# Moving the gate logits, the normalised rows and their stores from a stage of their own into the attention units

## What is computed

```python
x = x + _L1_xattn_ref(_layernorm(x), ctx_1024, ctx_1024, W_Query, W_Key, W_Value, W_Output, ...)
xf = _layernorm(x).reshape(N, D)               # N = 4096 tokens, D = 256
probs = softmax(xf @ gate_w.T)                 # 8 gate logits per token
scores_sel = _xmoe_route(probs)                # needs the probabilities of all tokens
y_e = gelu(xf @ w1[e].T) @ w2[e].T             # for each expert, capacity 512 tokens
x = x + sum over e of scores_sel[:, e] * y_e
```

## Time and profile before

| what | us |
|---|---|
| median of 3 runs (1861.0 to 1865.55) | 1862.72 |
| the profiled execution | 1861.19 |
| its span | 1859.5 |
| TensorE busy (91% of the span) | 1683.3 |
| VectorE busy (64%) | 1192.0 |
| ScalarE busy (45%) | 842.8 |
| GpSimd busy (33%) | 619.9 |

### The profile page before, as it was taken

One profiled execution on the slowest core, in us unless ns is written; L12 is line 12 of the kernel. 1 busy time (PEld: TensorE's weight loads), 2 busy tenths in 40 slices (PEclk: granted clock), 3 DMA queues, 4 the chain that ended last, 5 costly groups with the idle time before them and its releaser, 6 DMA issues. The chain is left out here.

```text
span 1859.5 us, 26060 instructions
## 1 busy us (share of the span) xinstructions
PE 1683.3 (91%) x8890; PEld 1152.6 (62%) x8890; DVE 1192.0 (64%) x2642; ACT 842.8 (45%) x1870; POOL 619.9 (33%) x746
## 2 busy tenths in 40 slices
PE   6469999996999999999999999999999999873584
PEld 4357777764666666666666666666666666572352
DVE  6444454432777777777777777777777777667761
ACT  3324443431555555555555555555555555421110
POOL 2154444430333232333333233232323232210375
PEclk9669999997999999999999999999999999955797
DMA  7100000003323222232323223232322223144144
GB/s 258 21 22 13 12 12 1 1 0 105 69 46 69 53 61 64 51 69 46 69 48 67 56 58 68 46 69 46 68 51 64 58 57 69 23 146 132 44 85 57
DMA packets 66657, 109.46 MB, mean 59 GB/s; under 512 B 16088, under 2 KB 48096, under 8 KB 66528
## 3 DMA queue, kind: packets, MB, share of 16 engines
q1 hardware_dynamic: 60384, 99.29, 21.8%
q0 software_dynamic: 6144, 8.52, 2.8%
HBM read 27.84 MB, written 12.85 MB: 22 GB/s over the span
## 5 line engine op out<-in xcount | busy, mean ns | idle before, releaser
L1030 POOL TENSOR_SCALAR at_Pr<-at_Pr,at_rinv 128x512 f32<-128x512 f32 x512 | 354.1, 692 | 826.7 <-DVE at_rinv L1057 826.7
L1009 ACT ACTIVATE at_Pr<-at_ps,at_nmax 128x512 f32<-128x512 f32 x512 | 352.0, 687 | 522.7 <-DVE at_nmax L1052 521.1
L1052 DVE TENSOR_REDUCE at_nmax<-at_ps 128x1 f32<-128x512 f32 x512 | 350.9, 685 | 139.0 <-PE at_ps L917 128.0
L917 PE MATMUL at_ps<-at_k,at_q 128*128 128x512 f32 x1024 | 420.8, 492 | 9.7 <-DMA at_k<-at_k_own 8.0
L928 PE MATMUL at_ps<-k_ident,at_Pr 128*128 128x128 f32 x2048 | 310.5, 274 | 4.0 <-POOL at_Pr L1030 4.0
L928 PEld LDWEIGHTS at_ps<-k_ident,at_Pr 128*128 128x128 f32 x2048 | 249.5, 140 | 93.2 <-POOL at_Pr L1030 32.8
L1064 DVE COPY at_PT<-at_ps 128x512 f32<-128x512 f32 x384 | 261.3, 681 | 0.0
L917 PEld LDWEIGHTS at_ps<-at_k,at_q 128*128 128x128 f32 x1024 | 174.6, 191 | 129.6 <-issue 120.1
L938 PE MATMUL at_ps<-at_PT,at_V 128*64 128x512 f32 x1024 | 233.8, 598 | 0.9 <-DVE at_PT L1064 0.9
L1057 DVE RECIPROCAL at_rinv<-at_rsum 128x1 f32<-128x1 f32 x512 | 83.3, 163 | 174.5 <-ACT at_Pr L1009 172.5
L938 PEld LDWEIGHTS at_ps<-at_PT,at_V 128*64 128x64 f32 x1024 | 67.7, 136 | 121.5 <-issue 120.3
(11 more groups left out here) (237 smaller groups left out, 2030.5 us busy)
## 6 DMA issues: line engine op xcount, KB each, us to landing
at_k<-at_k_own SPq DMA_DIRECT2D x256, 256.0 KB, 4.1
k_x<-in_x SPq DMA_DIRECT2D x8, 512.0 KB, 7.8
mg_ctx<-in_ctx SPq DMA_DIRECT2D x8, 512.0 KB, 8.0
mx_ctxn<-in_ctx SPq DMA_DIRECT2D x8, 512.0 KB, 3.9
rows<-lo_xn SPq DMA_DIRECT2D x8, 512.0 KB, 3.0
out<-k_x SPq DMA_DIRECT2D x1, 4096.0 KB, 14.6
r_w<-in_L_ffn_w SPq DMA_DIRECT2D x16, 256.0 KB, 5.6
mx_w<-in_L_ffn_w SPq DMA_DIRECT2D x2, 1024.0 KB, 9.8
```

The source lines that it names most:

```text
L917: ins = pe.matmul(ps[:, S_BANK + j % 2, :], q2[:, u % 2, h, q:q + P], k2[:, u % 2, h, part, :], start=part == 0, stop=part == 1)
L1009: act.activation(Pr[:, j % 4, :], ps[:, S_BANK + j % 2, :], ACT.Exp, bias=nmax[:, j % 4:j % 4 + 1], accum_out=rsum[:, j % 4:j % 4 + 1]).th ...
L1030: pool.tensor_scalar(Pr[:, n % 4, :], Pr[:, n % 4, :], rinv[:, n % 4:n % 4 + 1], 1.0, ALU.mult, ALU.mult).then_inc(s["pn"], 1)
L1052: dve.tensor_reduce(nmax[:, j % 4:j % 4 + 1], ps[:, S_BANK + j % 2, :], AX.X, ALU.max, negate=True).then_inc(s["nmax"], 1)
```

## The change

The block logits is gone. Its work for batch b is done in the units of batch b+1: routed(u, r) gives the batch whose step belongs to unit u, which is b = u // 8 - 1 if u % 8 == r. In unit 8b+9 (NORM) VectorE takes the statistics in slots 2 to 5 and finishes them in slot 6, and GpSimd the power after its last tile. In unit 8b+10 (APPLY) VectorE normalises in slots 2 to 5, into the part of ctxT_all that batch b no longer needs (semaphore xn). In unit 8b+11 (TURN) TensorE turns the rows in slots 3 and 7, into A_BANK + 1. ScalarE copies them in slot 4 and in slot 0 of the next unit. In unit 8b+12 (GATE) TensorE makes the gate matmuls in slots 3 and 7, and ScalarE copies the logits in slot 0 of the unit after. The key projection of two units gets a wait for these copies.

The SP queue stores the normalised rows of a batch and its part of out (two DMAs of 256 KB and one of 512 KB, waiting for xn) in its loop, at unit 8b+11. The gate weights are loaded already transposed, by two DMAs with one piece of 4 bytes per weight, where they were loaded by rows and turned by TensorE. The last batch has no units behind it, and its steps follow the loop. The zeros of the spare rows are made and stored in router, and experts waits for the semaphores of all stores (rows_in, landed).

```diff
-def attention(nc, c, x_all, xnT_all, ctxT_all, first, Wq, Wk, Wv, Wo):
+def attention(nc, c, x_all, xnT_all, ctxT_all, first, Wq, Wk, Wv, Wo, gate_w, lg, rows, rows_in, out, landed):
...
         rinv = sb("rinv", [P, 4], F32)
+        gT = sb("gT", [P, DC, E], F32)
+        stats = sb("stats", [P, TPB, 6], F32)
+        mv = sb("mv", [P, TPB, 2], F32)
+        ve = sb("ve", [P, TPB], F32)
+        rstd = sb("rstd", [P, TPB], F32)
-                 "pt_v pt_a pv oT y_ps x")
+                 "pt_v pt_a pv oT y_ps x gT stats mv ve rstd xn tx_ps xT l_ps lg")
...
             return 0 <= u < U
+        def routed(u, r):
+            return u // HP - 1 if u >= HP and u % HP == r else None
+        NORM, APPLY, TURN, GATE, LAST = 1, 2, 3, 4, B - 1
+        def x_tile(b, t):
+            return x_all[:, b * TPB + t:b * TPB + t + 1, :].rearrange("p a d -> p (a d)")
+        def xn_tile(b, t):
+            at = b * S + D * (t % 2)
+            return ctxT_all[:, t // 2, at:at + D]
...
                 sp.dma_start(wo_s[:, :, :], wo_dram).then_inc(first["loaded"], 16)
+                with nc.allow_non_contiguous_dma("8 gate weights per row"):
+                    for k in range(DC):
+                        sp.dma_start(gT[:, k, :], gate_w.rearrange("e (k p) -> p k e", p=P)[:, k, :]
+                                     ).then_inc(s["gT"], 16)
+                def store_rows(b):
+                    sp.wait_ge(s["xn"], b + 1)
+                    rv = rows.rearrange("(b k h p) d -> b p k h d", k=2, h=2, p=P)
+                    for k in range(2):
+                        sp.dma_start(rv[b, :, k, :, 0:D], ctxT_all[:, k, b * S:b * S + S].rearrange(
+                            "p (h d) -> p h d", d=D)).then_inc(rows_in, 16)
+                    sp.dma_start(out[0:N, :].rearrange("(b t p) d -> b p t d", p=P, t=TPB)[b],
+                                 x_all[:, b * TPB:(b + 1) * TPB, :]).then_inc(landed, 16)
                 for u in range(U):
+                    if routed(u, TURN) is not None:
+                        store_rows(routed(u, TURN))
...
                                          k_own[AD * h:AD * h + AD, :, :].bitcast(F32)).then_inc(s["k2"], 16)
+                store_rows(LAST)
...
                         wait_count(pe, s["kl"], u)
+                        if routed(u - 1, GATE) is not None:
+                            pe.wait_ge(s["xT"], DC * routed(u - 1, GATE) + DC)
+                        if routed(u - 1, GATE + 1) is not None:
+                            pe.wait_ge(s["lg"], routed(u - 1, GATE + 1) + 1)
...
                     ins.then_inc(s["y_ps"], 1)
+                def turn_rows(b, k):
+                    if k == 0:
+                        pe.wait_ge(s["xn"], b + 1)
+                    else:
+                        pe.wait_ge(s["xT"], DC * b + 1)
+                    for t in range(TPB):
+                        ins = pe.transpose(ps[:, A_BANK + 1, P * t:P * t + P], xn_tile(b, t)[:, P * k:P * k + P],
+                                           c["ident"][:, :])
+                    ins.then_inc(s["tx_ps"], 1)
+                def map_gates(b, half):
+                    if half == 0:
+                        pe.wait_ge(s["xT"], DC * b + DC)
+                    for t in (2 * half, 2 * half + 1):
+                        for k in range(DC):
+                            ins = pe.matmul(ps[:, A_BANK + 1, E * t:E * t + E],
+                                            xnT_all[:, k, b * S + P * t:b * S + P * t + P], gT[:, k, :],
+                                            start=k == 0, stop=k == DC - 1)
+                    if half:
+                        ins.then_inc(s["l_ps"], 1)
...
                             output(u - 1, j - 5)
+                        if j in (3, 7) and there(u):
+                            if j == 3 and there(u + 1) and u % HP in (TURN, GATE):
+                                pe.wait_ge(s["kl"], u + 2)
+                            if routed(u, TURN) is not None:
+                                turn_rows(routed(u, TURN), j // 4)
+                            if routed(u, GATE) is not None:
+                                if routed(u, GATE) == 0 and j == 3:
+                                    pe.wait_ge(s["gT"], 16 * DC)
+                                map_gates(routed(u, GATE), j // 4)
+                for k in range(DC):
+                    turn_rows(LAST, k)
+                for half in range(2):
+                    map_gates(LAST, half)
...
                                    ).then_inc(s["oT"], 1)
+                def keep_rows(b, k):
+                    act.wait_ge(s["tx_ps"], DC * b + k + 1)
+                    act.copy(xnT_all[:, k, b * S:b * S + S], ps[:, A_BANK + 1, :]).then_inc(s["xT"], 1)
+                def keep_logits(b):
+                    act.wait_ge(s["l_ps"], b + 1)
+                    act.copy(lg[:, b * TPB:(b + 1) * TPB, :],
+                             ps[:, A_BANK + 1, 0:TPB * E].rearrange("p (t e) -> p t e", e=E)).then_inc(s["lg"], 1)
...
                                            ).then_inc(s["exp"], 1)
+                        if j == 4 and routed(u, TURN) is not None:
+                            keep_rows(routed(u, TURN), 0)
+                        if j == 0 and routed(u, TURN + 1) is not None:
+                            keep_rows(routed(u, TURN + 1), 1)
+                        if j == 0 and routed(u, GATE + 1) is not None:
+                            keep_logits(routed(u, GATE + 1))
...
                                      ).then_inc(s["pt_a"], 1)
+                for k in range(DC):
+                    keep_rows(LAST, k)
+                keep_logits(LAST)
...
             def _(pool):
+                def spread(b):
+                    wait_apart(pool, s["ve"], b + 1)
+                    pool.tensor_tensor(rstd[:, :], ve[:, :], c["minus_half"][:, 0:TPB], ALU.pow
+                                       ).then_inc(s["rstd"], 1)
...
                                        ALU.mult, ALU.mult).then_inc(s["pn"], 1)
+                    if n % NBL == NBL - 1 and routed(n // NBL, NORM) is not None:
+                        spread(routed(n // NBL, NORM))
+                spread(LAST)
...
                     dve.tensor_tensor(xv, ps[:, Y_BANK - half, :], xv, ALU.add).then_inc(s["x"], 1)
+                def take_stats(b, t):
+                    if t == 0:
+                        dve.wait_ge(s["x"], 2 * HP * (b + 1))
+                    ins = dve.bn_stats(stats[:, t, :], x_tile(b, t))
+                    if t == TPB - 1:
+                        ins.then_inc(s["stats"], 1)
+                def finish_stats(b):
+                    wait_apart(dve, s["stats"], b + 1)
+                    for t in range(TPB):
+                        ins = dve.bn_aggr(mv[:, t, :], stats[:, t, :])
+                    ins.then_inc(s["mv"], 1)
+                    dve.wait_ge(s["mv"], b + 1)
+                    wait_count(dve, s["rstd"], b)
+                    dve.tensor_scalar(ve[:, :], mv[:, :, 1], LN_EPS, None, ALU.add).then_inc(s["ve"], 1)
+                def apply(b, t):
+                    if t == 0:
+                        dve.wait_ge(s["rstd"], b + 1)
+                    ins = dve.tensor_scalar(xn_tile(b, t), x_tile(b, t), mv[:, t, 0:1], rstd[:, t:t + 1],
+                                            ALU.subtract, ALU.mult)
+                    if t == TPB - 1:
+                        ins.then_inc(s["xn"], 1)
...
                                 keys(u + 1)
+                        if 2 <= j < 2 + TPB and routed(u, NORM) is not None:
+                            take_stats(routed(u, NORM), j - 2)
+                        if j == 2 + TPB and routed(u, NORM) is not None:
+                            finish_stats(routed(u, NORM))
+                        if 2 <= j < 2 + TPB and routed(u, APPLY) is not None:
+                            apply(routed(u, APPLY), j - 2)
...
                                 add_out(u - 1, 1)
+                for t in range(TPB):
+                    take_stats(LAST, t)
+                finish_stats(LAST)
+                for t in range(TPB):
+                    apply(LAST, t)
...
...
-def logits(nc, c, landed, x_all, gate_w, rows, lg, out, zeros):
...
-def router(nc, c, lg, rows, prob, chunk, slot_b, ew, w1T, w2T, prefetch):
+def router(nc, c, landed, out, zeros, lg, rows, prob, chunk, slot_b, ew, w1T, w2T, prefetch):
...
                 prefetch(sp)
+                sp.wait_ge(s["zero"], 1)
+                sp.dma_start(out[N:N + SPARE, :], zeros[:, :]).then_inc(landed, 16)
...
+                dve.memset(zeros[:, :], 0.0).then_inc(s["zero"], 1)
...
+                pool.wait_ge(rows_in, 16 * 2 * B)
...
-                pool.wait_ge(landed, 32)
+                pool.wait_ge(landed, 16 * (B + 1))
...
-            logits(nc, c, landed, x_all, a["L1_ffn_gate_w"], rows, lg, out, zeros)
```

(15 more changed lines are left out.)

115 lines of the change are left out of this document (removed).

## The result

The changed kernel takes 1911.25 us (median of 4, 1907.8 to 1912.07), the kernel before, run beside it on the same chip, 1861.86 us (median of 4, 1860.43 to 1865.55). The ratio is 1.0259, with a 95% interval of 1.0239 to 1.0279: the change makes the kernel 2.6% slower. The profiled execution took 1911.29 (span 1909.6) against 1861.19 (span 1859.5), so 50.1 us of span have to be found.

The account below looks back on a forecast made before the run. TensorE's pace was taken to bound the 64 attention units. From 1861.2 us, -37.6 for the stage removed, +2.4 for gate-weight loads and +94.2 for seven batches at 13.45 gave 1920.2; forecast 1920, range 1894 to 1938.

Parts of the forecast that it names:

- Part 1: Between the last addition to x and the router: the logits stage goes, leaving batch 7's 12.6 us chain; -37.6 us.
- Part 2: Ahead of unit 0's k2 copies in the SP queue: gate weights loaded transposed in 4-byte pieces cost +2.4 us, once.
- Part 3: TensorE in the attention units: transposes and gate matmuls add 2.65 us per batch, less 0.6 from a bubble, seven batches.
- Part 4: TensorE's key projections: waits for ACT's turned copy (1.0 us) and the logits copy (0.6), 1.6 us per batch.
- Part 5: Statistics, normalising and power on VectorE and GpSimd in the attention units cost nothing (0 to 0.5 us per batch).
- Part 6: Units 8b+11: stores waiting for xn in the SP queue hold the k2 copies, so TensorE stands 7.2 us per batch.
- Part 7: After each stand in the attention loop: TensorE's clock drops to 1.2 GHz, losing 2.6 us per batch.
- (a): Rival: no stall at the first scores of units 8b+11, so the kernel gets faster, 1851.6 us; chance 0.05.
- (b): Rival: the stall in units 8b+11 occurs but TensorE's clock stays up, 1902 us; chance 0.12.
- (c): Rival: stall and contention in the attention loop are dearer, over 16 us per batch, above 1938 us; chance 0.08.
- (d): Rival: the end is not shortened, batch 7's chain being as long as the removed stage, 1958 us; chance 0.01.
- (e): Rival: the additions cancel to no change, the stall in the loop being only some 1.5 us; chance 0.01.

Follow-up runs that it names:

- Experiment 6: Changed kernel with stores behind the k2 copies, ScalarE's second turned-half copy ahead of exp(0), gate-weight loads behind unit 0's copies: 1840.24 us, ratio 0.9885 to the kernel before.
- experiment 1: Changed kernel with each batch's stores issued after unit 8b+11's k2 copies instead of in front of them: 1848.07 us, ratio 0.9918 to the kernel before.
- experiment 2: Changed kernel with the wait for xn still ahead of unit 8b+11's k2 copies, but the three stores behind them: 1903.45 us in one execution.
- experiment 3: Changed kernel with only the 512 KB store of x to out ahead of the k2 copies, the normalised rows' stores behind: 1909.15 us in one execution.
- experiment 5: Changed kernel with unused identity transposes before the first score of units 8b+11: 48 of them 1908.1 us, 66 of them 1900.56 us (ratio 1.0205 to the kernel before).
- experiment 4: Changed kernel with the stores one unit later, behind the wait for unit 8b+12's keys and ahead of its k2 copies: 1847.8 us in one execution.

## Why the prediction was right, and where its terms were off

Predicted was 1920 us in a range of 1894 to 1938; measured are 1911.25. The direction, the cause and the place were right. Every sign that the prediction had named came, so the mechanism was right and not only the number; the number itself is closer than its terms are, since several errors cancel. The signs: seven waits of 6 to 8 us on the DMA of at_k at the first score of units 11, 19, ..., 59, 51 us in all; the clock down behind the stand (0.51 in batch 0, and TURN longer than 18.84 in all seven); the other units at 18.16; the GATE units 2.4 longer; the router 12.5 us after the last addition. Step by step:

- **Part 1, the stage goes:** -37.6 predicted, -38.0 measured. The chain was read link by link from the stage that went away, at its own half-clock durations, and the links shown came out within 0.1 us.
- **Part 2, the gate weights:** the wait of unit 0 went from 8.05 to 9.2, 1.1 us and not 2.4: mis-sized. Experiment 6 takes the loads away and wins back 0.5 of it. The same wait is 9.1 to 10.5 us in the seven executions that issue these loads ahead of the copies, so neither figure is their price alone. Unit 0 itself began about 4 us earlier in the kernel after (436.7 against 440.88 for its first projection). This is not the change: of the nine profiled executions three (after, experiments 1 and 6) begin it at 436.7 to 437.4 and six at 440.4 to 440.9, with the same code ahead. The traces show where: up to 114 us both kinds are within 1 us of each other, and at 195 us they are about 4 apart. From 119 to 130 us the granted clock was 0.69 in the kernel before (6.8 us at the half level, which loses 3.4 us of busy time) and 1.00 in the kernel after; all six late executions have 0.69 there and all three early ones 1.00. Why the clock differed stays open.
- **Part 3, TensorE's own work:** 2.65 less 0.6 predicted, 2.05. Measured: transposes 0.68 (of 0.9 and a bubble), and gates with their wait 2.40, of which 0.6 to 0.8 are the wait, so 1.6 to 1.8 the gates. Sum 2.3 to 2.5. The bubble gave back 0.2 to 0.4 and not 0.6: mis-sized.
- **Part 4, two new waits:** 1.6 predicted. The first is 0.59 by the waits view and 0.8 by taking it away (predicted 1.0). The second, the copy of the logits, is zero: the unit behind the GATE unit took 18.16. In unit 13 ScalarE's read for exp(0) ended at 706.43, the copy at 706.51, and TensorE came to the projection at 706.77. The step that failed: I took from the earlier trace rows that TensorE starts this projection 0.34 us ahead of the end of exp(0), and left out that the transposes or gates of slot 7 stand in its queue just before. In unit 13 it starts 0.34 behind that end. The same lateness would bring the first wait below 1.0.
- **Part 5, VectorE and GpSimd at nothing:** right, to 0.3 us in all. NORM units stay at 18.16 but for unit 57 (18.44), and in experiment 1 so do APPLY units.
- **Part 6, the stand:** 7.2 predicted, 7.34 measured, but by errors that cancel. The working was hold 7.2 less slack 2.8 plus stores 3.0, which is 7.4. Measured it is hold 6.8 less slack 1.9 plus 2.7 for the stores ahead, which is 7.6; this is by how much the score comes later, and the idle time in its row is 0.2 less (experiment 2). The slack was too large by 0.9, since the copies end with their landing and not with their data, and the hold and the stores were too large by 0.4 and 0.3. That the total fitted to 0.1 us is luck: alone it would have confirmed a wrong working, and the same working made the expectation of experiment 2 miss by 1.3 us.
- **Part 7, the clock:** 2.6 predicted, about 2.1 measured (1.4 to 3.0). The price was taken from one stand, that ahead of unit 0, and how long the clock stays low behind a stand differs: there it was 5.6 us (a mean of 0.72 in 457.93 to 467.93 before), in the loop 3.0 to 6.2, 4.3 on average. One place could give the mechanism, but not the mean of seven.
- **Not in the sum:** the last value matmuls took 5.28 us where before they took 3.65, at a clock that is partly half. That is half of the 3.2 us by which the stretch to the last addition is longer. The other half is the same thing one unit earlier: the value matmuls of unit 62 took 4.76 for 3.65 and the transposes beside them 1.11 for 0.66, where the granted clock fell to the half level from 1690.8 on for 3.4 us. The stretch is 46.6 to 48.3 us wherever the clock fell in it (experiments 1, 2, 3, 5 and 6 too), and 44.9 in the two executions in which it did not, that of the kernel before and that of experiment 4. As experiment 1 has no stand in the loop, the stands are not what starts it; what does was not tested.

In sum, the loop was over-priced by 6.6 us (94.2 against 87.6), and unit 0's start and the tail nearly cancel (-3.0 + 3.2, where +2.4 and 0 were put). The upper bound has a slip: its own high ends add up to 16.8 us per batch (2.9 + 1.9 + 8.8 + 3.2), not 15.7, which would be about 1944 and not 1937. It made no difference here.

The rivals: (a), no stand, 1851.6, is not what the change does, but experiment 1 builds its condition (the copies issued before xn) and gives 1848.07, with 3.1 us per batch where (a) had 3.65. (b), the same delay with the clock up, 1902, is built by experiment 5 (66 transposes, 1900.56). (c) wanted over 16 us per batch, and 12.5 were measured; the DMA view shows stores and copies one after the other. (d) and (e) are excluded by the ledger.

## What to carry to other kernels

A wait put into an in-order issuing queue is paid by everything behind it: before you move a store into such a queue, look up what is issued next there, who waits for that, and how much slack it has to its landing (not to the end of its data). Here the same stores, behind four copies and not ahead of them, are the difference between 2.6% slower and 0.8% faster. And take a sum apart by doses (0, half, all of the data) even when its total comes out right.

## What the runs showed of the hardware

- **The clock fell after short stands too.** In experiment 5 TensorE stood 2.0 to 2.5 us behind 5.4 us of transposes at full clock, and in five of seven places the granted clock went to the 1.2 GHz level all the same; with 7.4 us of transposes and 0.54 us of stand on average it stayed at 1.00 in all seven. Why the two places differ from the five stays open.
- **The low clock did not last equally long.** Behind the seven stands of the kernel after, all of 7.3 to 7.4 us, TensorE ran at the 1.2 GHz level for 3.0 to 6.2 us more.
- **Rates of two kinds of transfer.** The stores from SBUF to HBM moved at about 345 GB/s, the k2 copies within SBUF at about 200 to 210, so that 1 MB of the one takes 3.0 us and 1 MB of the other 5.0. The landing of a copy came some 0.7 us behind the end of its data (1526.4 and 1525.7).
- **Small loads were cheap.** With two loads of 1024 pieces of 4 bytes each ahead of unit 0's copies its wait was 1.1 us longer than before, and taking them away gave back 0.5: less than half of the 2.4 worked out from one such load behind a large one, with the differences between executions inside it.
